# A four-layer graph network on one core: self loops on VectorE, a bank copy ahead of late operands, count maxima and small vector work in other places

## The chip, the core and the metric

The kernel runs on one core of a Trainium2 chip. A core has TensorE (PE, matmuls; PEld are its weight loads), VectorE (DVE), ScalarE (ACT), GpSimd (POOL) and SyncE (SP, which issues DMAs). The metric is the device time of one execution in microseconds (us); lower is better.

## What is computed

`x` has 2048 nodes of 512 features. Four blocks follow one another, each on `relu(layernorm(x))` and added to `x`: an attention block, a block of three GCN layers with self loops and degree scaling, one GCN layer scaled by out degrees, and one layer with edge weights. Cut to what the change touches:

```python
def _gcn_norm(edge_index, n):
    loops = jnp.arange(n)                      # a self loop for each node
    row, col = concat(edge_index[0], loops), concat(edge_index[1], loops)
    deg = segment_sum(ones, col);  dis = rsqrt(deg)
    return row, col, dis[row] * dis[col]
def _gcn_layer(x, row, col, norm, W, b, n):
    h = x @ W
    return segment_sum(h[row] * norm[:, None], col, n) + b
h = relu(_gcn_layer(h, W1, b1));  h = relu(_gcn_layer(h, W2, b2));  h = _gcn_layer(h, W3, b3)
...
h = relu(_layernorm(x));  x = x + relu(segment_sum(norm * (h @ W.T + b)[row], col))
h = relu(_layernorm(x));  x = x + relu(segment_sum((h @ Wx)[col] * edge_weight, row))
```

## The kernel before

Since all edges share one index set, the kernel keeps a dense matrix `count` of how often an edge joins two nodes (16-bit, 128 partitions x 16 tiles x 2048) and turns each segment sum into matmuls with it. After the attention there are five "layers", numbered 0 to 4 in the code: three of the GCN block, the fourth with out degrees, and the one with edge weights.

**Products.** Each layer begins with `products(layer)`: 16 tiles of 128 nodes, each a product with the weights made of 12 matmuls of 128x512 (high and low halves of both operands). For tile t, ACT writes the high half of the input (`split_hi`), DVE the low half (`split_lo`), both into one of two slots of `h_parts`, and PE waits for the low half in `await_parts`, two matmuls before the end of the tile in front of it (in layers 1 and 2). In layer 2 the result is split by ACT and then by DVE (`product_lo`) into `g`. In layers 0 and 1 ACT evicts it to `h_gcn_t` and `operands` makes from it the parts of the half-size products.

**Half-size products.** In layers 0 and 1 the product with `count` is done in two halves h (a pair each) of seven steps of 32 matmuls by a Strassen-like scheme (`paired_sums`). Left operands are `A11`, `A12`, `A22` and the sums `S1` to `S4`, each in two quarters q, each with a high part (`operand_hi`, ACT) and a low part (`operand_lo`, DVE); `combine` (DVE) forms the sums. Right operands are `count` or mixtures of it in `mix` (`mix_two`, `mix_one`, `mix_three`, `mix_four`, DVE). Step 1's banks are copied out by ACT in `keep_first`; step 3 writes into them again and waits for it. `join`, `first_sum`, `second_sum` and `third_sum` (DVE) add banks and multiply by `dis_row`, the in-degree scale of each node. `relu_sums` (ACT) and `largest` (DVE) follow. From the maxima comes a common scale for the next layer: `pair_peak` (DVE) gives a column, `peak_row` (a PE transpose) turns it, `pair_scale` (some 15 tiny DVE instructions) makes powers of two of it, and `peak_all` (a PE matmul) spreads them. The next layer's products have begun by then, and PE meets both in its own queue.

**Sums.** Layers 2 and 3 use plain products with `count` (`sums`), four chunks c of four tiles, each finished by DVE in `finish`.

**Count maxima.** Layer 4 needs the largest entry of `count`, taken tile by tile by `count_peak` on DVE, before `edge_scale` in layer 3's sums.

Every engine runs its own queue in program order and waits on semaphores; all orders are written out by hand. So what stands ahead of an instruction in its queue delays it, whether it needs it or not.

## Time and profile before

| | |
|---|---|
| median of 3 runs | 1406.57 us (1406.09 to 1408.78) |
| the profiled execution's own time | 1407.51 us |
| its span in the trace | 1405.8 us |
| PE busy | 1342.7 us, 96% of the span |
| DVE busy | 952.9 us, 68% |
| ACT busy | 634.5 us, 45% |
| POOL busy | 98.3 us, 7% |

The span runs from the first to the last recorded instruction. The attention ends near 530 us. Layer 0's products run from 532 to 593 us, its half-size products to 698 us; layer 1's to 744 and 847 us; layer 2's products to 901 us and sums to 1022 us; layer 3's products to 1073 us. Matmuls are pipelined and their ends are modelled, so a matmul's printed duration is longer than the distance to the next one.

### The profile page before, as it was taken

To read this page: it belongs to the slowest core of one execution; us is meant where nothing else is said; L and a number is where in the kernel's file an instruction comes from. 1 tells how busy PE (TensorE), PEld (TensorE's weight loads), DVE (VectorE), ACT (ScalarE), POOL (GpSimd) and SP (SyncE) were. 2 spreads that over 40 slices of the span, in tenths; PEclk is the share of its full clock that TensorE was granted. 3 is DMA by queue.
4 is the path that set the end of the run, shared out by engine and by line. 5 is a ranking of instruction groups with operands and counts; after the bars stand their busy time and mean duration, and the time that the engine had idled before them with its cause. 6 is when DMAs were issued, how large, how long until landed. Compare 5 with 4: busy or idle time off the path is not lost.

```text
span 1405.8 us, 26594 instructions
## 1 busy us (share of the span) xinstructions
PE 1342.7 (96%) x11145; PEld 828.3 (59%) x11145; DVE 952.9 (68%) x1374; ACT 634.5 (45%) x1076; POOL 98.3 (7%) x102
## 2 busy tenths in 40 slices
PE   8889999989998998989998998899999999999998
PEld 8779898989996653534443443355444445444443
DVE  8998998999988885678768778833554323532322
ACT  2666566656554456743365434221253224422322
POOL 3120010101002213000000001002100000000000
PEclk9899999999999999999999999999999999999999
DMA  9634334435348721000000012022211222553201
GB/s 338 222 114 148 135 132 137 135 124 175 121 156 285 240 78 47 1 0 30 1 1 1 0 31 83 0 53 83 68 29 39 66 77 71 207 209 105 90 0 60
DMA packets 71333, 136.91 MB, mean 97 GB/s; under 512 B 11908, under 2 KB 24324, under 8 KB 69798
## 3 DMA queue, kind: packets, MB, share of 16 engines
q1 hardware_dynamic: 68542, 123.98, 26.8%
q0 software_dynamic: 1280, 5.77, 1.5%
q10 hardware_dynamic: 1384, 5.38, 1.1%
q8 instruction: 91, 1.49, 0.4%
q14 instruction: 36, 0.29, 0.1%
HBM read 81.79 MB, written 53.32 MB: 96 GB/s over the span
## 4 chain that ended last, share of the span: by engine, by line
PE 73%; DVE 21%; ACT 3%; issue 2%; DMA 1%; POOL 0%; ACTq 0%; DVEq 0%; SPq 0%; POOLq 0%
PE banks L2545 16%; PE banks L2607 11%; PE banks L2485 10%; PE banks L2420 10%; PE banks L1255 6%; PE banks L1659 3%; DVE x_sb L894 3%; PE banks L1192 3%; PE banks L1209 2%; PE banks L1266 2%; PE banks L1166 2%; DVE count_max L3018 2%; DVE x_sb L877 1%; PE banks L2357 1%; PE banks L1629 1%
## 5 line engine op out<-in xcount | busy, mean ns | idle before, releaser
L2420 PE MATMUL banks<-w_parts,h_parts 128*128 128x512 f16 x960 | 221.3, 384 | 15.4 <-DVE h_parts L2695 8.8
L2545 PE MATMUL banks<-g,count 128*128 128x512 f16 x1024 | 227.5, 379 | 0.5 <-DVE tiles L2986 0.5
L2420 PEld LDWEIGHTS banks<-w_parts,h_parts 128*128 128x128 f16 x960 | 91.2, 99 | 134.8 <-DVE h_parts L2695 14.7
L2545 PEld LDWEIGHTS banks<-g,count 128*128 128x128 f16 x1024 | 99.8, 98 | 113.7 <-DVE tiles L2986 1.0
L2607 PE MATMUL banks<-g,part 128*128 128x512 f16 x768 | 165.9, 379 | 0.0
L894 DVE TENSOR_TENSOR x_sb<-eb_parts,x_sb 128x4096 f16<-128x4096 f16 x64 | 145.9, 2279 | 0.0
L1255 PE MATMUL banks<-x_sb 128*128 128x128 f16 x2048 | 126.5, 220 | 12.3 <-DVE x_sb L894 12.2
L1255 PEld LDWEIGHTS banks<-x_sb 128*128 128x128 f16 x2048 | 120.4, 99 | 15.9 <-DVE x_sb L894 14.9
L2607 PEld LDWEIGHTS banks<-g,part 128*128 128x128 f16 x768 | 75.1, 98 | 90.6
L3069 DVE SCALAR_TENSOR_TENSOR part<-count,e_scale,part 128x1024 f16<-128x1024 f32 x29 | 37.2, 1284 | 105.9 <-ACT part L2307 105.9
L2307 ACT ACTIVATE part<-count,e_scale 128x1024 f16<-128x1024 f32 x29 | 33.3, 1149 | 110.9 <-PE banks L2607 110.9
L2697 DVE TENSOR_TENSOR h_parts<-h_gcn_t,h_parts 128x512 f16<-128x512 f32 x48 | 41.1, 862 | 55.4 <-ACT h_parts L2135 55.3
L877 DVE TENSOR_TENSOR x_sb<-iota_src,keys 128x2048 f16<-128x2048 f16 x64 | 77.6, 1213 | 0.0
L2485 PE MATMUL banks<-count,g 128*128 128x512 f16 x256 | 59.6, 392 | 7.7 <-ACT h_gcn_t L2217 7.7
L1266 PE MATMUL banks<-x_sb 128*128 128x64 f16 x1024 | 64.7, 190 | 0.0
L1267 PE MATMUL banks<-x_sb 128*128 128x32 f16 x1024 | 63.8, 177 | 0.0
L2230 ACT ACTIVATE h_gcn_t<-h_gcn_t,b_col,unscale 128x512 f32<-128x512 f32 x32 | 24.7, 807 | 86.4 <-DVE h_gcn_t L2904 44.4
L1266 PEld LDWEIGHTS banks<-x_sb 128*128 128x128 f16 x1024 | 60.4, 96 | 0.5
L1267 PEld LDWEIGHTS banks<-x_sb 128*128 128x128 f16 x1024 | 58.7, 96 | 0.1
L1659 PE MATMUL banks<-wo_sb,att_t 128*128 128x512 f32 x128 | 58.2, 597 | 0.4 <-ACT att_t L1567 0.4
L1006 ACT COPY bias<-banks 128x128 f32<-128x128 f32 x64 | 24.9, 388 | 72.3 <-PE banks L1255 72.2
L2485 PE MATMUL banks<-mix,g 128*128 128x512 f16 x256 | 56.9, 379 | 0.3 <-DVE mix L2809 0.3
(370 smaller groups left out, 2239.6 us busy)
## 6 DMA issues: line engine op xcount, KB each, us to landing
weight_dram<-w_new SPq DMA_DIRECT2D x60, 256.0 KB
count<-weight_dram SPq DMA_DIRECT2D x29, 512.0 KB, 7.0
qk_dram<-stage SPq DMA_DIRECT2D x64, 128.0 KB, 2.4
tiles<-x_dram SPq DMA_DIRECT2D x32, 256.0 KB, 3.5
x_dram<-tiles SPq DMA_DIRECT2D x32, 256.0 KB, 2.8
count<-in_x SPq DMA_DIRECT2D x4, 1024.0 KB, 13.0
h<-in_x SPq DMA_DIRECT2D x16, 256.0 KB, 4.6
h_dram<-h_t SPq DMA_DIRECT2D x8, 512.0 KB, 3.3
```

The costliest lines, as they stand in the source:

```text
L877: dve.tensor_tensor(m.hot_src[:, z].rearrange("p g (c two) -> p g c two", two=2), keep.iota_src[:].rearrange("p (c two) -> p c two", two=2 ...
L894: dve.tensor_tensor(m.hot_eb[:, z].rearrange("p g (t c) -> p g t c", t=NT), values, tiles, ALU.mult).then_inc(s["hots"], 1)
L1192: mm = pe.matmul(out, m.h_slab[slab % 2][:, zh, k, tile * P:(tile + 1) * P], keep.wq[:, zw, k, c * SCOLS:(c + 1) * SCOLS], start=n == 0, s ...
L1255: mm = pe.matmul(m.bias_ps[:, 0:NT * H], m.hot_src[:, z, g], parts[:, part], start=g == part == 0, stop=g == BATCH - 1 and part == 1)
L1266: pe.matmul(m.cw_ps[:, g, 0:2 * CCOLS], m.hot_src[:, z, g], m.hot_cw[:, z, g, 0:2 * CCOLS], start=True, stop=False)
L1267: mm = pe.matmul(m.cw_ps[:, g, CCOLS:2 * CCOLS], m.hot_src[:, z, g], m.hot_cw[:, z, g, 2 * CCOLS:CW], start=False, stop=True)
L1659: mm = pe.matmul(m.wo_ps[:, t % 2], m.att_t[:, k, :], keep.wo[:, k, :], start=k == 0, stop=k == KT - 1)
L2420: mm = pe.matmul(out, m.h_parts[:, slot, zh, k], m.w_parts[:, zw, k], start=n == 0 and layer != 3, stop=n == len(passes) - 1)
L2485: mm = pe.matmul(m.agg_ps[:, bank + d], left, right(i), start=new and i == 0 and z == 0, stop=i == HT - 1 and z == 1, skip_group_check=not ...
L2545: mm = pe.matmul(m.agg_ps[:, b], m.count[:, i, c, block], m.g[:, i, z], start=i == 0 and z == 0, stop=i == NT - 1 and z == 1)
L2607: mm = pe.matmul(m.banks[:, b], m.part[:, n % 3, z, b * P:(b + 1) * P], m.g[:, q, gz], start=q == 0 and (z, gz) == (0, 0), stop=q == NT - ...
L2697: dve.tensor_tensor(out, source, hi, ALU.subtract).then_inc(s["lo"], 1)
```

## The change

The change makes no instruction disappear except POOL's: it moves work between queues and within them.

- The 16 additions of self loops into `count` go from POOL to DVE (`add_loop`), two at each of the first eight tiles of layer 0's products.
- In `keep_first` of the first pair, ACT's copy stands ahead of the high parts of `A22` and `S4` (second quarters), which stood ahead of it.
- `mix_two` of layer 1 goes from tiles 10 and 11 to tiles 3 and 6; in layer 0 from 10 and 11 to 10 and 12. The low part of `A22` goes one tile later.
- `dis_row` is written in node order, so that it is read without a stride.
- In the second pair of layers 0 and 1, the two first input tiles of the next layer are split earlier, on ACT and on DVE; `peak_all` goes from step 4 to step 3.
- In the products of layers 1 and 2, `peak_row` goes from tile 1, matmul 4 to tile 2, matmul 0, and `peak_all` from tile 2, matmul 8 to matmul 11.
- `count_peak`: of 16, 11 stood in layer 2's products and 5 in its sums; now 5, 8, and 3 in layer 3's products.

```diff
-def layers_pool(nc, m, s, attended, ident):
+def layers_pool(nc, m, s, attended):
...
-    for t in LOOP_ORDER:
-        first = 2 * t % GPC
-        diag = m.count[:, t, t // PER].rearrange("p (v g) -> p g v", g=GPC)[:, first:first + 2]
-        pool.tensor_tensor(diag, diag, ident[:].rearrange("p (g v) -> p g v", g=2), ALU.add).then_inc(s["looped"], 1)
...
+    def add_loop(t):
+
+        first = 2 * t % GPC
+        diag = m.count[:, t, t // PER].rearrange("p (v g) -> p g v", g=GPC)[:, first:first + 2]
+        dve.tensor_tensor(diag, diag, keep.ident[:].rearrange("p (g v) -> p g v", g=2), ALU.add).then_inc(s["looped"], 1)
...
+            if layer == 0 and t < HT:
+                for i in (2 * t, 2 * t + 1):
+                    add_loop(LOOP_ORDER[i])
...
-               13: OPERANDS[6:7], 14: OPERANDS[7:8], 15: OPERANDS[8:]}
+               13: OPERANDS[6:7], 14: OPERANDS[7:8], 15: OPERANDS[8:12]}
...
         act.copy(by_graph(nodes(m, h, 0)), bank_pair(m, 2 * h)).then_inc(s["kept"], 1)
+        if h == 0:
+            for name, q in OPERANDS[12:]:
+                operand_hi(layer, name, q)
...
-    return m.dis_row[:, c * COLS:(c + 1) * COLS].rearrange("p (v g) -> p g v", g=GPC).unsqueeze(1).to_broadcast([P, n, GPC, GN])
+    return m.dis_row[:, c * COLS:(c + 1) * COLS].rearrange("p (g v) -> p g v", g=GPC).unsqueeze(1).to_broadcast([P, n, GPC, GN])
...
-            act.wait_ge(s["fin"], done + 1)
-            relu_sums(layer, h, (0, 1))
             if h == 1:
                 split_hi(layer + 1, 0)
                 split_hi(layer + 1, 1)
+            act.wait_ge(s["fin"], done + 1)
+            relu_sums(layer, h, (0, 1))
...
-            if layer in (1, 2) and (t, n) == (1, 4):
+            if layer in (1, 2) and (t, n) == (2, 0):
                 peak_row()
-            if layer in (1, 2) and (t, n) == (2, 8):
+            if layer in (1, 2) and (t, n) == (2, 11):
                 peak_all()
...
-        if (number, i) == ((5, 4) if h == 0 else (4, 4)):
+        if (number, i) == ((5, 4) if h == 0 else (3, 6)):
             peak_all()
...
+        if layer and t in (3, 6):
+            mix_two(layer, 0, t // 6)
...
-            if layer == 2 and 5 <= t < 5 + EARLY_PEAKS:
-                count_peak(t - 5)
+            if layer == 2 and t in (5, 7, 9, 11, 13):
+                count_peak((t - 5) // 2)
+            if layer == 3 and t in (6, 8, 10):
+                count_peak(NT - 3 + (t - 6) // 2)
...
-            for i in ((), (0, 1), (2, 3, 4), ())[c]:
-                count_peak(EARLY_PEAKS + i)
+            for i in ((5, 6), (7, 8, 9), (10, 11, 12), ())[c]:
+                count_peak(i)
```

The first place is DVE's queue at the start of layer 0's products. Before (`h_parts` is the low half of an input tile, `rstd` the variance step of the layer norm):

```order
L1736 TENSOR_SCALAR rstd<-stats_106 128x3
L3071 MEMSET b_ones 33x64
L3073 MEMSET b_ones 1x128 x2
L2697 TENSOR_TENSOR h_parts<-h_gcn_t,h_parts 128x512 x4
L1741 RECIPROCAL rstd<-rstd 128x3
```

and of the change:

```order
L1736 TENSOR_SCALAR rstd<-stats_106 128x3
L3080 MEMSET b_ones 33x64
L3082 MEMSET b_ones 1x128 x2
L2770 TENSOR_TENSOR count<-count,ident 128x2x64 x2
L2696 TENSOR_TENSOR h_parts<-h_gcn_t,h_parts 128x512
L2770 TENSOR_TENSOR count<-count,ident 128x2x64 x2
L2696 TENSOR_TENSOR h_parts<-h_gcn_t,h_parts 128x512
```

Two additions now stand ahead of each of the low halves, from tile 2 on.

The second place is ACT's queue at the end of layer 0's products. The casts (L2174, L2169) are the high parts of operands, `g` that of `A22` and `S_1_0_90` that of `S4`; the copy (L2217, L2213) is `keep_first`. Before:

```order
L2174 CAST S_0_0_88<-h_gcn_t 128x1024
L2174 CAST S_1_0_82<-h_gcn_t 128x1024
L2174 CAST g<-h_gcn_t 128x4x256
L2174 CAST S_1_0_90<-h_gcn_t 128x1024
L2217 COPY h_gcn_t<-banks 128x2x512
L2224 ACTIVATE banks,stats_78<-count 128x1024 x4
```

and of the change:

```order
L2169 CAST S_0_0_88<-h_gcn_t 128x1024
L2169 CAST S_1_0_82<-h_gcn_t 128x1024
L2213 COPY h_gcn_t<-banks 128x2x512
L2169 CAST g<-h_gcn_t 128x4x256
L2169 CAST S_1_0_90<-h_gcn_t 128x1024
L2223 ACTIVATE banks,stats_78<-count 128x1024 x4
```

The copy has moved ahead of the last two casts. The same happens in layer 1.

The third place is DVE's queue in layer 2's products (`g` is `product_lo`, `count_max` is `count_peak`). Before:

```order
L2695 SCALAR_TENSOR_TENSOR h_parts<-h_gcn_t,h_scale,h_parts 128x512
L2765 SCALAR_TENSOR_TENSOR g<-banks,g_scale,g 128x512
L3018 TENSOR_REDUCE count_max<-count 128x1
L2695 SCALAR_TENSOR_TENSOR h_parts<-h_gcn_t,h_scale,h_parts 128x512
L2765 SCALAR_TENSOR_TENSOR g<-banks,g_scale,g 128x512
```

and of the change:

```order
L2694 SCALAR_TENSOR_TENSOR h_parts<-h_gcn_t,h_scale,h_parts 128x512
L2764 SCALAR_TENSOR_TENSOR g<-banks,g_scale,g 128x512
L3027 TENSOR_REDUCE count_max<-count 128x1
L2694 SCALAR_TENSOR_TENSOR h_parts<-h_gcn_t,h_scale,h_parts 128x512
L2764 SCALAR_TENSOR_TENSOR g<-banks,g_scale,g 128x512
L2694 SCALAR_TENSOR_TENSOR h_parts<-h_gcn_t,h_scale,h_parts 128x512
L2764 SCALAR_TENSOR_TENSOR g<-banks,g_scale,g 128x512
L3027 TENSOR_REDUCE count_max<-count 128x1
```

A maximum now follows every second tile, not every tile.

## Rows read from the trace of the kernel before

**Rows 1.** Page, part 1: busy us of each engine (share of the span) and instructions.

```profile
PE 1342.7 (96%) x11145; PEld 828.3 (59%) x11145; DVE 952.9 (68%) x1374; ACT 634.5 (45%) x1076; POOL 98.3 (7%) x102
```

**Rows 2.** PE's waits, whole span: who waits for whom: us, times, longest.

```profile
PE banks L2420 <- DVE h_parts L2695: 8.8, 11, 1.5
...
PE banks L2485 <- DVE mix L2809: 0.3, 2, 0.2
```

**Rows 3.** Timelines, 530 to 549 us, start of layer 0: start, us, instruction [idle before].

```profile
532.77 9.82 POOL L2066 TENSOR_TENSOR count<-count,ident 128x128 f16<-128x128 f16 x16
...
536.46 6.16 DVE L1736 TENSOR_SCALAR rstd<-stats 128x3 f32<-128x3 f32 x1
...
543.13 1.29 DVE L2697 TENSOR_TENSOR h_parts<-h_gcn_t,h_parts 128x512 f16<-128x512 f32 x2
...
543.88 5.12 PE L2420 MATMUL banks<-w_parts,h_parts 128*128 128x512 f16 x12 [5.47 <-DVE h_parts L2697]
```

**Rows 4.** Windows: length; busy of PE, PEld, DVE, ACT, POOL; PE's granted clock, DMA.

```profile
543.88:548.84 4.96, 4.96 (x12) 1.85 (x13) 0.54 (x1) 0.00 (x0) 0.00 (x0) 0.51 0.00 0
762.30:769.21 6.91, 6.91 (x32) 3.14 (x33) 4.62 (x3) 4.44 (x8) 0.00 (x0) 1.00 0.00 0
852.63:857.86 5.23, 5.23 (x18) 1.93 (x16) 4.07 (x15) 0.72 (x1) 4.47 (x4) 0.69 0.93 306
```

**Rows 5.** Timelines of ACT and PE, steps 2 and 3, layers 0 and 1.

```profile
603.12 1.04 ACT L2174 CAST S<-h_gcn_t 128x1024 f16<-128x1024 f32 x1 [0.21 <-DVE h_gcn_t L2778]
...
610.24 1.01 ACT L2217 COPY h_gcn_t<-banks 128x1024 f32<-128x1024 f32 x1
...
611.30 9.86 PE L2485 MATMUL banks<-count,g 128*128 128x512 f16 x32 [3.80 <-ACT h_gcn_t L2217]
...
762.30 7.08 PE L2485 MATMUL banks<-count,g 128*128 128x512 f16 x32 [3.85 <-ACT h_gcn_t L2217]
```

**Rows 6.** Timelines of PE and DVE, first tiles of layer 1.

```profile
698.36 3.83 PE L2420 MATMUL banks<-w_parts,h_parts 128*128 128x512 f16 x17
...
704.03 0.16 DVE L2727 TENSOR_REDUCE peak<-h_max 128x1 f32<-128x5 f32 x1
...
704.24 0.27 PE L2363 MATMUL banks<-ident,peak 128*1 128x128 f32 x1 [2.05 <-DVE peak L2727]
...
706.87 0.75 DVE L2695 SCALAR_TENSOR_TENSOR h_parts<-h_gcn_t,h_scale,h_parts 128x512 f16<-128x512 f32 x1 [0.21 <-ACT h_parts L2133]
```

**Rows 7.** Timelines of PE, ACT and DVE in layer 2's products.

```profile
866.74 2.76 PE L2420 MATMUL banks<-w_parts,h_parts 128*128 128x512 f16 x12 [0.47 <-DVE h_parts L2695]
...
867.45 0.72 ACT L2133 ACTIVATE h_parts<-h_gcn_t,h_scale 128x512 f16<-128x512 f32 x1 [1.94 <-PE banks L2420]
...
869.46 0.74 DVE L2695 SCALAR_TENSOR_TENSOR h_parts<-h_gcn_t,h_scale,h_parts 128x512 f16<-128x512 f32 x1
...
898.36 3.19 PE L2420 MATMUL banks<-w_parts,h_parts 128*128 128x512 f16 x14 [0.75 <-DVE h_parts L2695]
```

**Rows 8.** Timelines of DVE and PE in layer 3's products.

```profile
1042.56 0.75 DVE L2765 SCALAR_TENSOR_TENSOR g<-banks,g_scale,g 128x512 f16<-128x512 f32 x1 [1.11 <-ACT g L2161]
...
1044.26 1.09 DVE L2697 TENSOR_TENSOR h_parts<-h_gcn_t,h_parts 128x512 f16<-128x512 f32 x1 [0.95 <-ACT h_parts L2135]
...
1045.41 0.39 PE L2416 MATMUL banks<-b_parts,b_ones 33*128 33x512 f16 x1 [0.15 <-DVE h_parts L2697]
...
1055.94 0.75 DVE L2765 SCALAR_TENSOR_TENSOR g<-banks,g_scale,g 128x512 f16<-128x512 f32 x1 [1.11 <-ACT g L2161]
...
1058.13 0.39 PE L2416 MATMUL banks<-b_parts,b_ones 33*128 33x512 f16 x1
```

**Rows 9.** DVE's groups by shape, 530 to 910 us: busy us, mean ns.

```profile
L3018 DVE TENSOR_REDUCE count_max<-count 128x1 f32<-128x2048 f16 x11 | 25.0, 2274 | 0.0
...
L2900 DVE TENSOR_TENSOR h_gcn_t<-banks,h_gcn_t 128x1024 f32<-128x1024 f32 x16 | 19.5, 1220 | 6.5 <-PE banks L2485 5.0 <-ACT h_gcn_t L2217 1.5
...
L2904 DVE TENSOR_TENSOR h_gcn_t<-h_gcn_t,dis_row 128x1024 f32<-128x1024 f32 x8 | 16.2, 2021 | 0.3
```

More of the change, by code:

```diff
@@ L1796 @@
 FIN = (0, 10, 20, 20 + NT, 20 + 2 * NT)
-EARLY_PEAKS = 11
 LOOP_ORDER = tuple(range(PER)) + tuple(range(HT, HT + PER)) + tuple(range(PER, HT)) + tuple(range(HT + PER, NT))
@@ L2204, in products @@
                 act.wait_ge(keep.attention_sems["dis_made"], c + 1)
-                act.copy(m.dis_row[:, c * COLS:(c + 1) * COLS], m.agg_ps[:, c]).then_inc(keep.attention_sems["dis_rowed"], 1)
+                act.copy(m.dis_row[:, c * COLS:(c + 1) * COLS].rearrange("p (g v) -> p g v", g=GPC),
+                         m.agg_ps[:, c].rearrange("p (v g) -> p g v", g=GPC)).then_inc(keep.attention_sems["dis_rowed"], 1)
             if layer == 4 and t == 1:
@@ L2790, in mix_two @@
         tiles = slice(PER * part, PER * (part + 1))
+        if layer == 0:
+            dve.wait_ge(s["looped"], HT * (h + 1))
         if h:
@@ L2830, in operands @@
             combine(layer, "S3", 1)
-        if t == 10:
-            if layer == 0:
-                dve.wait_ge(s["looped"], HT)
-            mix_two(layer, 0, 0)
+        if layer == 0 and t in (10, 12):
+            mix_two(layer, 0, t // 12)
         if t == 11:
             operand_lo(layer, "S3", 1)
-            mix_two(layer, 0, 1)
         if t == 12:
@@ L2841, in operands @@
             combine(layer, "S2", 0)
+        if t == 14:
             operand_lo(layer, "A22", 0)
-        if t == 14:
             combine(layer, "S1", 0)
@@ L2948, in paired_sums @@
             mix_three(layer, h, 3)
+            if h == 1:
+                split_lo(layer + 1, 0)
+                split_lo(layer + 1, 1)
             dve.wait_ge(s["joined"], 6 * number + 1)
@@ L2956, in paired_sums @@
                 weight_spread(layer + 1)
-            else:
-                split_lo(layer + 1, 0)
-                split_lo(layer + 1, 1)
             largest(layer, h, "C11")
@@ L2963, in paired_sums @@
             if h == 0:
-                if layer == 0:
-                    dve.wait_ge(s["looped"], NT)
                 mix_two(layer, 1, 0)
@@ L3117, in graph_layers @@
     layers_act(nc, keep, m, s, tools.act)
-    layers_pool(nc, m, s, attended, keep.ident)
+    layers_pool(nc, m, s, attended)
     layers_pe(nc, keep, m, s, tools.pe)
```

## Prediction, made before the change was run

> **What bounds the kernel now.** I read the page first: PE is busy for 96% of the span and no other engine for more than 68% [rows 1]. The change takes no matmul away, so it can only win what PE loses by waiting or by running at the lower clock. The list of PE's waits shows whose these are; the reader should see that DVE's low halves cost 8.8 us in eleven waits, the longest 1.5 us [rows 2]. Then I went through the timelines of the stages that the diff touches, and through windows for the clock. In window 762.30 a step's 32 matmuls start within 6.91 us at full clock [rows 4], 0.216 us each, so a product of 12 takes 2.59 us. Printed idle time begins at a modelled end that lies 0.16 to 0.17 us behind the next possible start, so each wait costs that much more than printed. The waits to look at:
>
> - 5.47 us in layer 0's products [rows 3].
> - 3.80 and 3.85 us for ACT's copy before step 3, layers 0 and 1 [rows 5].
> - 2.05 us for the maximum at the start of layer 1 [rows 6], and its like in layer 2.
> - A wait of 0.75 us before each product of layer 2 [rows 7].
>
> **Self loops.** DVE's variance step, 128x3 numbers, takes 6.16 us and ends at 542.62; POOL's sixteen additions end at 542.59 [rows 3]. DVE was held by POOL, not by its own work, and the low half that PE waits for stands behind it. PE then starts at 543.88 and its 12 matmuls take 4.96 us with a granted clock of 0.51, the lower level of 1.2 GHz [rows 3, 4]: 2.37 us more than 2.59. The place costs 5.64 + 2.37 = 8.0 us. With POOL's additions gone the step is a fraction of a microsecond. Two additions now stand ahead of the low half. No row shows one on DVE. POOL's took 0.61 (9.82/16) [rows 3], the upper bound. By elements alone, at the rate of a multiplication with a strided operand (2.02 us for 1024) [rows 9], it is 0.25, the lower bound, and a fixed part comes on top. I take 0.4, nearer to the vector row, and 0.8 for two. DVE's low half came 0.51 us after the step's end [rows 3]; so it would come at about 536.6 + 0.5 + 0.8 = 537.9 and be done at 538.6, where PE is free at 538.24 (the wait's beginning less the modelled part). **Gain 7.6**, with 7.2 to 7.9 by the bounds. The other fourteen lie in DVE's waits for ACT, in tiles where PE needs 2.59 us and DVE some 2.
>
> A rule bears on the cause. The Trainium skill, "GPSIMD Engine Reference", section 8 (Key points), says that GpSimd shares its SBUF interfaces with VectorE, which clash when VectorE runs in a two-port mode or has two SBUF inputs. The trace agrees as to the first: the held step has one input. By its second half the additions themselves would be safe now that POOL is idle there; the sum is unchanged.
>
> **The copy ahead of late operands.** PE waits for the copy, which ends at 611.25; it stands behind two casts that wait for DVE's sums. The last cast that stays ahead begins at 603.12 and takes 1.04 [rows 5], so the copy can run from 604.2 to 605.2. PE's step 2 ends at 607.34 (611.30 less 3.96), 2 us later: the wait goes whole. What is late next? `A22`'s cast comes after the copy, at 605.2 to 606.2; DVE, busy until then, takes it at 607. The mixture and the join for step 4 follow, needed seven microseconds later. Layer 0: 3.96, and its step 3 takes 9.86 printed where the like one takes 7.08 [rows 5], 2.78 more by the clock. Layer 1: 4.01 and no clock. **Gain 10.7.**
>
> **Mixtures earlier.** The longest wait for a low half, 1.55 us, comes at layer 1's tile behind two mixtures. Two instructions of 1.22 us, moved to tiles with room, leave some 0.2 at each of two places: **gain 1.3**. In layer 0 the move only shifts a wait; nothing.
>
> **Scale chain.** Reading `dis_row` without a stride should bring 2.02 down to the 1.22 of a join of the same shape [rows 9]. Eight such and others shorten DVE's chain at the end of a layer, where DVE is busy throughout. The maximum then comes some 3 us after step 7's end, not at 704.2, which is 5.8 after it (698.36) [rows 6]. PE turns it after 25 matmuls, 5.4 us: no wait. But the chain of tiny instructions keeps its length: from the transpose at 704.24 to the low half of tile 3 at 706.87, which takes 0.75 [rows 6], 3.4 us; 0.4 less without the wait and idle time in it is not sure, so 3.2. PE gets only nine matmuls, 2.0 us, behind the transpose before it needs this low half. A new wait of 1.2 us takes the place of 2.2: **gain 1.0**. In layer 2 the same, and there 16 matmuls of the old row lie in a window at clock 0.69 and take 5.23 [rows 4] where 3.5 is normal: 1.7 more; POOL's bias additions slow DVE there and take some back. **Gain 2.2.** The lower bound is nothing at both, if the new wait grows to the old one. The two small waits for `mix` (0.3 printed) [rows 2], with the modelled part: **0.6**.
>
> **Count maxima.** Ten starts of PE from 866.74 to 898.36 are 3.51 us apart [rows 7], not 2.59: 0.92 lost at each of nine, 0.64 at the first, 8.9. A maximum takes 2.27 [rows 9], about 2.19 start to start. Let PE pass the gate of tile t at 0. ACT starts the next high half at 0.71, DVE could start the low half at 1.46 (0.75 later) and takes 0.74; PE wants it at 2.59. `product_lo` follows at 2.1, a maximum runs from 2.8 to 5.0, so the low half of the tile after next ends at 5.77, wanted at 5.18. A wait of 0.6 then, and the tile without a maximum lets DVE catch up. Five: 3.0. **Gain 5.9.** The eight in the sums lie in waits of 5 us and more.
>
> The three in layer 3 are not free. There `product_lo` starts at 1042.56 and is through at 1043.2; a maximum ends at 1045.4; the low half that began at 1044.26 and took 1.09 ends at 1046.5, and PE, which started at 1045.41, had already waited for it [rows 8]. 1.1 lost, the same at tile 8. At tile 10 the maximum begins at 1056.6 and ends at 1058.8, the low half at 1059.9, against a start at 1058.13 without a wait [rows 8]: 1.8. **Loss 4.0.** Nothing at the one end, 3 x 2.2 = 6.6 at the other.
>
> **Sum.** 7.6 + 10.7 + 1.3 + 1.0 + 2.2 + 0.6 + 5.9 - 4.0 = 25.3. The profiled execution took 1407.51 us (a span of 1405.8 and 1.7 around it), 0.9 above the median of the runs shown. 1407.5 - 25.3 = 1382.2, and on the median's footing 1381.3.
>
> **Rivals.**
>
> *The clock falls elsewhere.* Three of the waits were followed by slow matmuls, 1.7 to 2.8 us each (6.8 in my sum); of the waits of 3.96 and 4.01 us one was and one was not [rows 4, 5]. New waits of 1.2 to 1.8 us stay. If one or two of them meet a fall: 1384 to 1389. Against it: ten waits of 0.75 in a row met none.
>
> The Trainium skill, "TensorE: Matmul & The Clock Gate", Part 1 (What's actually happening), says that the array's default is the throttled state and that work lifts it, judged on a free-running basis. By that rule the same wait may or may not cost, as rows 5 show.
>
> *Maxima hidden.* If DVE has more room than I count, five or all of the waits in layers 2 and 3 are smaller: 3 to 7 us more, 1374 to 1378. For it: the gaps are fractions of a microsecond. Against: each instruction in the count has a row.
>
> *Another wait replaces the copy's.* If the casts now behind the copy hold step 4, 8 of the 10.7 go: 1389 to 1391. Against: 7 us of room.
>
> *No change.* The moves shift waits only. That needs all of the above to fail; 1406.
>
> *Slower.* One mechanism: PE stays at 1.2 GHz behind the short waits left in the products, where ten are (five of 0.6, three in layer 3, two at the scale chain). A product at the lower level costs 2.37 more [rows 3, 4]. It decides from twelve slow products on (25.3 + 2.8 = 28.1): 1409.5 and more. Against it, the trace has eleven waits for low halves [rows 2], and the ten of layer 2 ran at full clock.
>
> **How the numbers follow.** The forecast has 0.60 (1377 to 1386), the clock elsewhere 0.15, maxima hidden 0.13, another wait 0.05, still larger gains 0.02, no change 0.02, slower 0.03. From the forecast's range I reach to most of the clock's cases and to the hidden maxima: 1375 to 1389 holds a little over 8 in 10. A measurement of this kernel can tell about 0.2% (2.8 us) from no change. Faster by more: 0.95; within: 0.02; slower by more: 0.03.
>
> **What would show it.** Right: `rstd`'s step at 0.2 us and no wait of PE behind it; step 3 directly behind step 2 in both layers; multiplications with `dis_row` at 1.22; PE waiting near 1.2 us for tile 3's low half, not for the maximum; five waits of 0.6 in layer 2 and three of 1.1 to 1.8 in layer 3. Wrong: an addition of more than 0.6 us, new windows with a clock under 1.00 behind the new waits, a wait of PE for `joined` before step 4, or layer 3's products no longer than before.

## The result

The changed kernel takes 1385.36 us (median of 4 runs, 1381.71 to 1386.9), the kernel before beside it 1407.67 (4 runs): a ratio of 0.984 (0.981 to 0.986). Run again beside other kernels it took 1384.17 (5 runs), against 1407.65 (9 runs): 0.983 (0.982 to 0.985). The prediction was 1381.3 in a range of 1375 to 1389, with 0.95 on faster by more than 0.2%.

The page's first part of the changed kernel: PE's busy time is 4 us shorter (fewer slow matmuls) and its idle time some 16 us [rows 1].

```profile
PE 1338.9 (97%) x11145; PEld 829.4 (60%) x11145; DVE 944.3 (68%) x1390; ACT 636.0 (46%) x1076; POOL 90.1 (7%) x86
```

PE's waits, whole span of the changed kernel (us, times, longest):

```profile
PE banks L2415 <- DVE h_parts L2696: 4.6, 5, 1.7
PE banks L2419 <- DVE h_parts L2694: 4.4, 7, 1.3
...
PE banks L2419 <- DVE h_parts L2696: 1.3, 2, 0.7
```

The 8.8 us in eleven waits of [rows 2] have become 4.4 in seven, and those for `mix` are gone. The group at L2415, the bias matmul that opens a product of layer 3, has grown to 4.6 us; in the kernel before it was

```profile
PE banks L2416 <- DVE h_parts L2697: 0.6, 4, 0.2
```

The start of layer 0 in the timelines of DVE and PE (start, us, instruction, idle before):

```profile
539.46 0.17 DVE L1736 TENSOR_SCALAR rstd<-stats 128x3 f32<-128x3 f32 x1
540.18 1.30 DVE L2770 TENSOR_TENSOR count<-count,ident 128x128 f16<-128x128 f16 x2
541.10 0.89 DVE L2696 TENSOR_TENSOR h_parts<-h_gcn_t,h_parts 128x512 f16<-128x512 f32 x1
542.05 2.76 PE L2419 MATMUL banks<-w_parts,h_parts 128*128 128x512 f16 x12 [0.56 <-DVE h_parts L2696]
```

`rstd`'s step takes 0.17 us instead of 6.16, PE waits 0.56 instead of 5.47, and its product takes 2.76 instead of 5.12 [rows 3]. Two additions take 0.92 from start to start.

ACT and PE around step 3 of layer 0:

```profile
599.80 1.04 ACT L2169 CAST S<-h_gcn_t 128x1024 f16<-128x1024 f32 x1 [0.22 <-DVE h_gcn_t L2783]
600.76 1.01 ACT L2213 COPY h_gcn_t<-banks 128x1024 f32<-128x1024 f32 x1
601.66 1.05 ACT L2169 CAST g<-h_gcn_t 128x1024 f16<-128x1024 f32 x1
...
603.30 7.07 PE L2484 MATMUL banks<-count,g 128*128 128x512 f16 x32
```

The copy stands behind the cast that was ready, PE's step 3 has no idle time and takes 7.07 where it took 9.86 [rows 5].

The start of layer 1's products, PE and DVE. The maximum is there 3.2 us after step 7's end (687.24), 2.2 before the transpose; the chain of tiny steps then runs to the low half of tile 3, for which PE waits:

```profile
687.24 5.56 PE L2419 MATMUL banks<-w_parts,h_parts 128*128 128x512 f16 x25
690.46 0.16 DVE L2726 TENSOR_REDUCE peak<-h_max 128x1 f32<-128x5 f32 x1
692.63 0.27 PE L2362 MATMUL banks<-ident,peak 128*1 128x128 f32 x1
693.84 0.16 DVE L2638 TENSOR_SCALAR line<-line 1x2 int32<-1x2 int32 x1
694.57 0.22 DVE L2743 TENSOR_SCALAR line<-h_line,line 1x2 f32<-1x2 f32 x1
695.57 0.60 PE L2419 MATMUL banks<-w_parts,h_parts 128*128 128x512 f16 x2 [0.72 <-DVE h_parts L2694]
```

The same place in layer 2, where GpSimd adds biases meanwhile: the second 1x2 step takes 0.65 for 0.22, and PE waits longer.

```profile
833.89 5.58 POOL L2066 TENSOR_TENSOR tiles<-tiles,b_row 128x512 f32<-128x512 f32 x4 [298.01 <-DMA tiles<-x_dram]
834.92 0.26 DVE L2638 TENSOR_SCALAR line<-line 1x2 int32<-1x2 int32 x1
835.75 0.65 DVE L2743 TENSOR_SCALAR line<-h_line,line 1x2 f32<-1x2 f32 x1
837.18 0.60 PE L2419 MATMUL banks<-w_parts,h_parts 128*128 128x512 f16 x2 [1.25 <-DVE h_parts L2694]
```

A maximum in layer 2's products, and the third one in layer 3's, DVE and PE:

```profile
849.43 2.28 DVE L3027 TENSOR_REDUCE count_max<-count 128x1 f32<-128x2048 f16 x1
851.62 0.74 DVE L2694 SCALAR_TENSOR_TENSOR h_parts<-h_gcn_t,h_scale,h_parts 128x512 f16<-128x512 f32 x1
852.42 5.35 PE L2419 MATMUL banks<-w_parts,h_parts 128*128 128x512 f16 x24 [0.43 <-DVE h_parts L2694]
...
1032.86 2.27 DVE L3027 TENSOR_REDUCE count_max<-count 128x1 f32<-128x2048 f16 x1
1035.05 1.06 DVE L2696 TENSOR_TENSOR h_parts<-h_gcn_t,h_parts 128x512 f16<-128x512 f32 x1
1036.17 0.39 PE L2415 MATMUL banks<-b_parts,b_ones 33*128 33x512 f16 x1 [1.72 <-DVE h_parts L2696]
1036.49 4.45 PE L2419 MATMUL banks<-w_parts,h_parts 128*128 128x512 f16 x12
```

In each the low half stands directly behind the maximum and PE behind it. Behind the 1.72 us the twelve matmuls start over 4.38 us instead of 2.7; the window of them, in which the third number from the end is PE's granted clock, 0.62:

```profile
1036.49:1040.94 4.45, 4.45 (x14) 1.58 (x13) 1.27 (x2) 0.00 (x0) 0.00 (x0) 0.62 0.00 0
```

The two groups by shape on DVE that the prediction priced (530 to 890 us; busy us, mean ns):

```profile
L2770 DVE TENSOR_TENSOR count<-count,ident 128x128 f16<-128x128 f16 x16 | 10.4, 844 | 0.0
...
L2915 DVE TENSOR_TENSOR h_gcn_t<-h_gcn_t,dis_row 128x1024 f32<-128x1024 f32 x8 | 9.8, 1225 | 0.3
```

(Instructions without a wait between them overlap as printed, so 844 is not the distance between two additions.) The multiplication takes 1.225 us instead of 2.021 [rows 9].

Where the time went, by stages. Each length is the distance from PE's first matmul of the stage to that of the next one, in the timeline of one profiled execution (the bias matmul of 0.32 us that opens layer 3's products counts to the sums ahead of it); "again" is the changed kernel's second profile.

| stage | before | after | again | gain | predicted |
|---|---|---|---|---|---|
| layer 0, products | 61.33 | 54.21 | 54.21 | 7.1 | 7.6 |
| layer 0, steps | 104.84 | 97.76 | 97.75 | 7.1 | 6.7 + 0.3 |
| layer 1, products | 46.11 | 43.32 | 43.32 | 2.8 | 1.3 + 1.0 |
| layer 1, steps | 102.10 | 97.75 | 97.75 | 4.35 | 4.0 + 0.3 |
| layer 2, products | 54.82 | 47.07 | 48.84 | 7.75; 5.98 | 2.2 + 5.9 |
| layer 2, sums | 121.25 | 121.24 | 121.24 | 0.0 | 0 |
| layer 3, products | 50.47 | 56.21 | 54.52 | -5.74; -4.05 | -4.0 |
| all of these | 540.92 | 517.56 | 517.63 | 23.4; 23.3 | 25.3 |

What lies ahead is untouched and varies: the first product started at 532.19 before, 535.27 after and 530.87 again, and between 530.2 and 533.1 in the profiles of the experiments. What lies behind layer 3's products took 332.7, 332.8 and 332.7 us. So a single execution's time can stand some 3 us off for reasons outside the change, and in what follows the verdicts rest on stages where less than that is asked.

### The profile page after: what moved, and what is told of

The parts are those of the page before. It is cut to its first block, busy times and chain, and to the rows that moved or that the text cites. A ratio compares the mean times of both kernels' runs of the same rounds, so it can differ in the third digit from the quotient of the medians.

```text
span 1385.6 us, 26596 instructions
## 1 busy us (share of the span) xinstructions
PE 1338.9 (97%) x11145; PEld 829.4 (60%) x11145; DVE 944.3 (68%) x1390; ACT 636.0 (46%) x1076; POOL 90.1 (7%) x86
## 4 chain that ended last, share of the span: by engine, by line
PE 81%; DVE 13%; ACT 3%; issue 2%; DMA 1%; POOL 0%; ACTq 0%; DVEq 0%; SPq 0%; POOLq 0%
PE banks L2544 16%; PE banks L2484 14%; PE banks L2606 12%; PE banks L2419 11%; PE banks L1255 6%; PE banks L1659 4%; DVE x_sb L894 3%; PE banks L1192 3%; PE banks L1209 2%; PE banks L1266 2%; PE banks L1166 2%; DVE count_max L3027 1%; PE banks L2356 1%; DVE x_sb L877 1%; PE banks L1629 1%
## 5 line engine op out<-in xcount | busy, mean ns | idle before, releaser
L2484 PE MATMUL banks<-mix,S 128*128 128x512 f16 x256 | 56.8, 379 | 0.0
```

Of the source, the lines that this page charges most:

```text
L2484: mm = pe.matmul(m.agg_ps[:, bank + d], left, right(i), start=new and i == 0 and z == 0, stop=i == HT - 1 and z == 1, skip_group_check=not ...
```

## Experiments

"Before +" and "after +" say which of the two kernels was edited. Stage lengths are measured as above.

**The copy alone (before +).**

```diff
-               13: OPERANDS[6:7], 14: OPERANDS[7:8], 15: OPERANDS[8:]}
+               13: OPERANDS[6:7], 14: OPERANDS[7:8], 15: OPERANDS[8:12]}
...
         act.copy(by_graph(nodes(m, h, 0)), bank_pair(m, 2 * h)).then_inc(s["kept"], 1)
+        if h == 0:
+            for name, q in OPERANDS[12:]:
+                operand_hi(layer, name, q)
```

> The kernel before with one edit: ACT's copy of step 1's banks ahead of the high parts of A22 and S4 (second quarters), in layers 0 and 1. My theory: the two waits of PE for the copy (3.96 and 4.01 us with the modelled part) go whole and the slow matmuls behind the first of them too, so layer 0 from step 1 to step 4 takes 20.7 us instead of 27.48 and layer 1 20.7 instead of 24.74; 10.8 us in all, 0.992 of the time before. Rival one: the casts now behind the copy hold step 4 or later, so that less than 3 us is left and the difference shows as a new wait in steps 4 to 7 (77.36 us before in each layer). Rival two: the clock falls at the same place without the wait, layer 0 then takes 23.5 us.

Measured: 1396.81 us (4 runs) against 1408.2 (7 runs), ratio 0.991 (0.988 to 0.994). The steps of layer 0 went from 104.84 to 98.08, those of layer 1 from 102.10 to 98.08; every other stage is within 0.25 of before. The waits for the copy are gone and none takes their place: 10.8 us by the two stages. The medians differ by 11.4, and the ratio's interval is 8.6 to 16.8 us. It is the largest part of the change, in four lines.

**Self loops back on GpSimd (after +).**

```diff
+    for t in LOOP_ORDER:
+        ...
+        pool.tensor_tensor(diag, diag, ident[:].rearrange("p (g v) -> p g v", g=2), ALU.add).then_inc(s["looped"], 1)
...
-            if layer == 0 and t < HT:
-                for i in (2 * t, 2 * t + 1):
-                    add_loop(LOOP_ORDER[i])
```

> The changed kernel with the sixteen self loops back on POOL at their old place. My theory: DVE's variance step (128x3) is held until POOL's last addition ends, about 6 us instead of 0.17, PE's wait in front of its third product grows from 0.56 to about 5.5 us and slow matmuls follow; from the first product of layer 0 to the start of the fourth 17.5 us instead of 10.26, everything else as in the changed kernel, so about 7.3 us more. Rival: the step was long because of what stood around it on DVE and ACT, not because of POOL; then the step stays at 0.2 us and the stage at 10 to 11 us.

Measured: 1388.07 us in one run; layer 0's products 60.52 instead of 54.21, 6.3 more (about 7.3 expected). Timelines of GpSimd, DVE and PE:

```profile
531.92 9.79 POOL L2065 TENSOR_TENSOR count<-count,ident 128x128 f16<-128x128 f16 x16
...
535.58 6.15 DVE L1736 TENSOR_SCALAR rstd<-stats 128x3 f32<-128x3 f32 x1
...
543.00 4.19 PE L2423 MATMUL banks<-w_parts,h_parts 128*128 128x512 f16 x12 [5.45 <-DVE h_parts L2700]
```

The hold is back, to the end of GpSimd's run of additions, as in [rows 3]; only the slow matmuls behind it cost 1.4 us this time where they had cost 2.4. Layer 3's products took 54.53 here: the three waits and no slow product.

**Self loops on GpSimd, but after the second product (after +).** As before, with one more line ahead of the loop.

```diff
+    pool.wait_ge(s["prod"], 2)
     for t in LOOP_ORDER:
```

> The changed kernel with the self loops on POOL, but started only when two products of layer 0 are done, so that they lie behind DVE's variance step. My theory: what counts is the overlap with a DVE step that has one input in SBUF, not the engine that adds. The variance step takes 0.2 us, PE's wait of 0.56 goes to near zero, DVE's low halves are slower while POOL works (about 1.0 us instead of 0.69), and the reciprocal of 128x3 behind them is held until POOL's end. First product to fourth 9.5 to 10.5 us, the whole within 1 us of the changed kernel. Rival: sixteen additions on POOL cost PE some 7 us wherever they stand while layer 0's products run; 1.5% of nothing saved, 7 us more than the changed kernel.

Measured: 1384.08 us in one run; layer 0's products 53.47, 0.7 less than the changed kernel's 54.21. GpSimd and DVE:

```profile
539.32 10.04 POOL L2066 TENSOR_TENSOR count<-count,ident 128x128 f16<-128x128 f16 x16 [5.70 <-PE banks L2424]
...
546.02 0.96 DVE L2701 TENSOR_TENSOR h_parts<-h_gcn_t,h_parts 128x512 f16<-128x512 f32 x1 [2.66 <-ACT h_parts L2135]
546.91 0.16 DVE L1741 RECIPROCAL rstd<-rstd 128x3 f32<-128x3 f32 x1
```

What was to be avoided was the meeting of `rstd`'s TENSOR_SCALAR with the additions, not GpSimd as such: with the run elsewhere PE doesn't wait for its third product at all, since no additions stand ahead of the low half. I had expected the RECIPROCAL on the same 128x3 numbers to be held in its turn. It wasn't: 0.16 us in the middle of the run. The low halves, with two inputs, took up to 0.96 instead of 0.69 beside it.

**Node order alone (before +).**

```diff
-    return m.dis_row[:, c * COLS:(c + 1) * COLS].rearrange("p (v g) -> p g v", g=GPC).unsqueeze(1)...
+    return m.dis_row[:, c * COLS:(c + 1) * COLS].rearrange("p (g v) -> p g v", g=GPC).unsqueeze(1)...
...
-                act.copy(m.dis_row[:, c * COLS:(c + 1) * COLS], m.agg_ps[:, c])...
+                act.copy(m.dis_row[:, c * COLS:(c + 1) * COLS].rearrange("p (g v) -> p g v", g=GPC),
+                         m.agg_ps[:, c].rearrange("p (v g) -> p g v", g=GPC))...
```

> The kernel before with one edit: dis_row in node order. My theory: its multiplications take 1.22 us instead of 2.02 and 0.69 instead of 1.09, DVE's chain at the end of layers 0 and 1 gets 2.4 us shorter, and PE's wait of 2.05 us (2.2 with the modelled part) for the maximum goes in both; with the transpose at its old place the low half of tile 3 comes in time as well, so layer 1's first three products end 8.4 us after step 7, not 10.5, and layer 2's 8.4 to 9, not 12.2. 4.4 to 6 us in all. That would be as much as the changed kernel gets there (1.7 and 2.9) although it moved the transpose as well. Rival: the chain is bound by ACT's relus and PE's steps; then the multiplications are shorter but the maximum comes less than 1 us earlier and PE's wait stays over 1 us.

Measured: 1404.03 us in one run; layer 1's products 44.08 (46.11 before), layer 2's 52.27 (54.82). DVE and PE, start of layer 1 (step 7 ended at 698.10):

```profile
701.73 0.16 DVE L2728 TENSOR_REDUCE peak<-h_max 128x1 f32<-128x5 f32 x1
...
701.95 0.27 PE L2364 MATMUL banks<-ident,peak 128*1 128x128 f32 x1
```

The maximum comes at 3.6 us instead of 5.7 [rows 6], and PE doesn't wait for it even with the transpose at its old place. So the order of nodes alone brings 2.0 and 2.55 us, which is more than the whole chain brought in layer 1 in the change (below).

One stage got longer without an edit in it: layer 1's steps took 103.46 us (102.10 before). PE's wait for the copy is that of before, but this time its step 3 was slow:

```profile
760.00 8.77 PE L2486 MATMUL banks<-count,g 128*128 128x512 f16 x32 [3.85 <-ACT h_gcn_t L2218]
```

It took 7.08 behind the same wait in [rows 5], so the wait that the prediction priced without slow matmuls can have them too.

**Strided order again (after +).** The reverse edit.

> The changed kernel with the in-degree scale written and read in the old, strided order again; nothing else is changed. My theory (with the transpose later, the maximum has slack): the multiplications take 2.02 us again instead of 1.22, the maximum of layer 1 comes about 1.5 us later (4.7 instead of 3.2 us after step 7's end), still ahead of the transpose at 5.4, and the products of layers 1 and 2 stay at 43.3 and 47.1 us, the steps at 97.8: no change of more than 0.3. Rival: the order is what brought the gain at the end of the layers: the transpose waits again, and each of the two stages is 1 to 3 us longer.

Measured: 1381.12 us in one run; layer 1's products 43.82 (43.32), layer 2's 47.52 (47.07; 48.84 again), the steps 97.75. The multiplications took 2.02 us as expected, but there is a new wait. DVE and PE:

```profile
686.52 0.16 DVE L2725 TENSOR_REDUCE peak<-h_max 128x1 f32<-128x5 f32 x1
686.59 0.74 DVE L2693 SCALAR_TENSOR_TENSOR h_parts<-h_gcn_t,h_scale,h_parts 128x512 f16<-128x512 f32 x1
...
687.39 0.82 PE L2418 MATMUL banks<-w_parts,h_parts 128*128 128x512 f16 x3 [0.30 <-DVE h_parts L2693]
```

The transpose doesn't wait, as I had said, but tile 2's low half stands behind the maximum in DVE's queue and is now late: 0.5 us in layer 1. My expectation of no change over 0.3 missed that by 0.2, the rival's 1 to 3 us by more. With the later transpose the order of nodes is worth 0.5 us in layer 1; with the old one 2.0. Layer 2 has the new wait too (0.32), but its stage differs by more than that among kernels that do the same there (47.07 to 48.91), so its length settles nothing. The two edits cover the same wait, and where both are made the later transpose only makes the chain end later.

**The transpose six matmuls earlier, the spreading four (after +).**

```diff
-            if layer in (1, 2) and (t, n) == (2, 0):
+            if layer in (1, 2) and (t, n) == (1, 6):
                 peak_row()
-            if layer in (1, 2) and (t, n) == (2, 11):
+            if layer in (1, 2) and (t, n) == (2, 7):
                 peak_all()
```

> The changed kernel with the transpose of the maximum six matmuls earlier (tile 1, matmul 6; it was tile 2, matmul 0) and the spreading four earlier (tile 2, matmul 7). Theory (the chain's length from the transpose is fixed, so PE's wait for tile 3's low half shrinks by what the transpose is earlier, 1.3 us, as long as the maximum is there): layer 1's products 43.3 to 42.4, the wait of 0.72 gone; layer 2's 47.1 to 45.8, the wait of 1.25 at 0.2 or less. Rival (the maximum is not there yet): a wait of PE for the maximum comes in its place and the stages stay at 43.3 and 47.1.

Measured: 1379.86 us in one run. Layer 1's products 42.43, no wait left; layer 2's 46.34, with two waits, 0.56 for the chain and 0.20 for the low half, in place of the 1.25 or 2.1. As the theory has it in layer 1 (42.4), 0.5 short of it in layer 2 (45.8). The transpose at tile 2, matmul 0 was later than the maximum needs.

**Three maxima out of layer 3's products (after +).**

```diff
-            if layer == 3 and t in (6, 8, 10):
-                count_peak(NT - 3 + (t - 6) // 2)
...
+            if layer == 2 and c and b == 1:
+                count_peak(12 + c)
```

> The changed kernel with the three count maxima of layer 3's products moved into layer 2's sums, one in each of the last three chunks; those of layer 2's products stay. Theory: the three maxima are the whole loss of layer 3's products: they take 50.5 us (before: 50.5), instead of 56.2, and layer 2's sums stay at 121.2. Rival (the loss has another part, such as split work moved there, or the maxima cost as much in the sums): layer 3's products stay over 51.5, or the sums grow by over 1 us.

Measured: 1378.72 us in one run; layer 3's products 50.47, layer 2's sums 121.24. Four starts of PE at L2415 still show 0.15 to 0.16 of idle time, as in [rows 8], and none more. The loss in layer 3 was the three maxima and what followed them, nothing else.

**All sixteen in layer 2's sums (after +).** The five of layer 2's products go too: three behind each of the first three chunks, seven inside the last three.

> The changed kernel with all 16 count maxima in layer 2's sums, none in the products. Theory: layer 2's products go from 47.1 to about 43.9 (five waits of 0.42 to 0.75 printed go, each with 0.16 of the modelled end), layer 3's from 56.2 or 54.5 to 50.5, sums stay 121.2. Rival (a maximum in the sums delays finish): sums over 122 and layer 3's first products later.

Measured: 1377.33 us in one run. Layer 3's products 50.47 and sums 121.25 as expected. Layer 2's products 45.97, not 43.9: the wait for tile 3's low half was 2.18 in this execution and the matmuls behind it were slow (the first 34 took 8.77 us at a granted clock of 0.81, where they take 7.51 at 1.00). The comparison of the two kernels with the earlier transpose, with and without the five maxima (46.34 here above, 43.10 below), is free of that: 3.24 us for the five.

**Both together (after +).** All sixteen in the sums, transpose and spreading earlier.

> The changed kernel with all 16 count maxima in layer 2's sums and none in the products of layers 2 and 3, and with the transpose of the maximum at tile 1, matmul 6 and the spreading at tile 2, matmul 7. My theory (what is left of the loss is DVE's maxima ahead of low halves, and the scale chain counted from the transpose): layer 3's products 50.5 us instead of 56.2 (three waits and one slow product gone), layer 2's products about 3.0 to 3.3 shorter by the maxima and 1 to 1.4 by the chain (43 us), layer 1's products 0.9 shorter (42.4), layer 2's sums unchanged at 121.2; together 9 to 11 us below the changed kernel where its clock fell, 8 to 9 where it did not: a median near 1376, ratio to before 0.977. Rival: the maxima are not free in the sums either (16 x 2.2 us on DVE, with finish behind them), so the sums grow by 2 us or more and the total stays above 1380.

**The changed kernel again, in the same group of runs.**

> The changed kernel itself, unchanged, beside the others on the same chip. Theory: 1382 to 1386, ratio 0.982 to 0.985; layer 3's products are 54.5 us (three waits alone) or 56.2 (with one slow product): by the theory that the clock's fall comes and goes from execution to execution, either may stand here. Rival: the fall belongs to this kernel and stands there each time (56.2).

Measured: both together 1373.83 us (5 runs), ratio to before 0.976 (0.975 to 0.978); the changed kernel 1384.17, ratio 0.983. Layer 1's products 42.43, layer 2's 43.10, sums 121.24, layer 3's products 50.48. A median of 1376 was expected: 2 us better than that.

In the changed kernel's second profile layer 3's products took 54.52, so the slow product of the first belongs to an execution, not to the kernel. Layer 2's products took 48.84, 1.8 more than in the first. DVE and PE there:

```profile
830.51 1.08 DVE L2638 TENSOR_SCALAR line<-line 1x2 int32<-1x2 int32 x1
...
833.60 0.60 PE L2419 MATMUL banks<-w_parts,h_parts 128*128 128x512 f16 x2 [2.08 <-DVE h_parts L2694]
...
834.65 8.92 PE L2419 MATMUL banks<-w_parts,h_parts 128*128 128x512 f16 x34
```

The 1x2 step took 1.08 us, not 0.26, the wait grew by as much, and the 34 matmuls behind it took 8.92 against 7.86. What decides it is how far GpSimd's additions have come when the step is due. GpSimd at that moment:

```profile
830.31 1.26 POOL L2066 TENSOR_TENSOR tiles<-tiles,b_row 128x512 f32<-128x512 f32 x1
```

This addition ends at 831.57, the step, which began at 830.51, at 831.59. In the first profile an addition ran from 833.89 to 835.16 and the step from 834.92 to 835.18: it came up near the addition's end. In each of the twelve profiles that have the additions beside this step, it ends within 0.03 us of the end of an addition, after 0.26 to 1.19 us. The second 1x2 step ends with the next addition and takes 0.65 each time. The first profile's 0.26 was the exception among the changed kernel and those edits of it that leave the transpose in place: the wait of PE was 1.25 us there, 1.82 in one and 2.08 to 2.18 in five others. This led to the last two kernels.

**GpSimd's first four bias additions after layer 2's products (after +).**

```diff
+    pool.wait_ge(s["prod"], 3 * NT)
     for t in range(NT):
         b = t % PER
         pool.wait_ge(s[f"in_x{b}"], 16 * (t // PER + 1))
         pool.tensor_tensor(m.tiles[:, b], m.tiles[:, b], m.b3_row[:], ALU.add).then_inc(s["plus"], 1)
```

> The changed kernel, but GpSimd's first four bias additions (5.6 us, which begin 5.2 to 5.6 us after layer 2's products) wait until those products are done; they are needed some 20 us after that. Theory (these additions hold DVE's tiny one-input steps on 1x2 numbers, 0.65 for 0.22 and up to 1.2 for 0.16 us, and so make PE's wait at tile 3 of layer 2 1.25 to 2.1 us instead of layer 1's 0.72): the two steps take 0.16 and 0.22 us, the wait is 0.72, and layer 2's products take 46.3 to 46.6 us (47.1 to 48.8 with the additions there); the sums stay at 121.2. Rival (what stretches the chain in layer 2 is something else, such as its own instructions or a DMA): the steps stay long and the wait over 1.2.

Measured: 1382.78 us in one run. Layer 2's products 45.94 (47.07 and 48.84). DVE, PE and GpSimd:

```profile
832.02 0.16 DVE L2639 TENSOR_SCALAR line<-line 1x2 int32<-1x2 int32 x1
...
832.74 0.22 DVE L2744 TENSOR_SCALAR line<-h_line,line 1x2 f32<-1x2 f32 x1
...
833.74 0.61 PE L2420 MATMUL banks<-w_parts,h_parts 128*128 128x512 f16 x2 [0.72 <-DVE h_parts L2695]
...
871.66 4.95 POOL L2067 TENSOR_TENSOR tiles<-tiles,b_row 128x512 f32<-128x512 f32 x4 [338.69 <-PE banks L2420]
```

Both steps as short as in layer 1, and the wait to the hundredth that of layer 1. The stage is 0.4 us below the 46.3 to 46.6 expected: the `g_scale` step (128x16 numbers, right behind the chain) took 0.17 us as in layer 1, where the changed kernel's took 1.18, and the 34 matmuls behind the wait took 7.51 instead of 7.86. The sums stayed at 121.25. Layer 3's products took 56.11, with a slow product behind the 1.72 again.

**The same with both improvements.**

> The version with all maxima in the sums and the earlier transpose, and GpSimd's first four bias additions after layer 2's products. Theory: layer 2's products take 42.2 to 42.5 us like layer 1's 42.43 (43.10 with the additions there), all else the same: a median of 1373 to 1374 us, which 3 rounds can't tell from 1373.83; the stage can. Rival: the additions run into the sums' first finish instead and layer 2's sums grow past 121.5.

Measured: 1371.06 us (4 runs, 1370.29 to 1371.77) against 1407.9 (7 runs), ratio 0.974 (0.972 to 0.976). Layer 2's products 41.96, the shortest of all and 0.2 under what was expected; sums 121.25, layer 3's products 50.51. The median is 2 us under the 1373 to 1374 expected. After the chain PE shows no idle time:

```profile
830.15 0.38 PE L2370 MATMUL banks<-line,ones 1*128 1x8 f32 x2
830.47 34.71 PE L2420 MATMUL banks<-w_parts,h_parts 128*128 128x512 f16 x160
```

The profiled executions of the two versions took 1373.25 and 1370.85 us. Of these 2.4 us, 1.1 are in this stage and 1.3 ahead of the first product (530.89 against 532.23), where nothing was changed; so 1.1 is what the edit is shown to bring. It is the fastest version found: 13 us below the changed kernel, by nothing but places in queues.

## Why the prediction was right, point by point

The forecast was 1381.3 and the medians 1385.4 and 1384.2. 1.1 us of the difference is its footing (1406.57 of three runs; nine gave 1407.65), 2.0 are terms: 1407.65 - 23.3 = 1384.4. The first median lies 1.0 above that, in a group whose four runs differ by 5.2.

The two profiles miss the 25.3 by the same 2.0, but not by the same term. In the first it is nearly all the slow product behind a maximum in layer 3 (1.7), in the second the scale chain in layer 2 (2.1). That they agree is luck.

- **Self loops**, 7.6 predicted. The first three products take 10.26 us instead of 17.52: 7.26. The wait left is 0.56 printed; an addition costs 0.46 and not 0.4, and the low half behind two of them took 0.89 instead of 0.69. 0.14 went at a later tile. That GpSimd's additions held DVE's step is shown by putting them back and by putting them elsewhere.
- **The copy**, 10.7 predicted, 10.8 alone. Slow matmuls were put at 2.8 behind the wait in layer 0 and at nothing in layer 1; the node-order kernel had 2.9 and 1.7. What I said would be late next, `A22`'s cast and the mixture for step 4, was not.
- **Mixtures and chain in layer 1**, 1.3 + 1.0 predicted, 2.8 measured. No wait is left at the mixtures' new tiles. The node-order kernel, which has the wait behind the mixtures and no other, takes 44.08, the one without any wait 42.43: 1.65. The chain's part is then 1.15. Both parts are differences between kernels; the mixtures were not moved alone, nor were the two earlier splits and the earlier `peak_all` of the half-size products, so their shares stay open. The new wait, 0.72 printed and 0.89 with the modelled part, is worth what the earlier transpose gained, 0.89. Its size was put at 1.2: the chain from the transpose to the end of the low half was put at 3.2 us and took 2.9 (692.63 to 695.51).
- **The chain in layer 2**, 2.2 predicted with nothing as the lower bound. From the shortest length of this stage, 41.96, before lost 12.86, of which 8.9 to the maxima; the changed kernel lost 5.11, of which 3.26 to its five waits (2.46 printed and five times 0.16). Chain and slow matmuls went from 4.0 to 1.85: a gain of 2.1. In the second profile the same subtraction (6.88, less 2.93) leaves 3.95 and no gain at all. Over the seven profiles with GpSimd's additions and the transpose in place, it leaves a gain of 2.1 once, 1.4 to 1.6 twice and none four times. So the 2.2 fits the first profile by luck, and the lower bound, nothing, is the commoner case. I wrote that the bias additions "take some back" without pricing how long one of them holds a 1x2 step.
- **Small mix waits**, 0.6 predicted, 0.65 (97.76 against the copy alone's 98.08, twice). They are gone with the order of nodes alone, and stay gone with the old order in the changed kernel, so more than one of the edits removes them.
- **Maxima in layer 2**, 5.9 predicted. 8.9 before; 3.24 after, by the pair of kernels with and without them: 5.7. Five waits of 0.6, as written (0.43 printed, 0.59 with the modelled part); in the first profile one of them was 0.75 printed, where `g_scale` was held.
- **Maxima in layer 3**, -4.0 predicted (1.1, 1.1, 1.8). The waits are 1.29, 1.29 and 1.72 printed, where 0.15 stood at the first two before; the stage lost 4.05, and 1.7 more where one product was slow. The kernel without them shows all of it.

Of the rivals, *the clock falls elsewhere* came true at one place in the first profile (1.7 us behind the 1.72 us wait) and at another in the second (behind the 2.08). *Maxima hidden* is refuted by the two kernels with maxima moved, *another wait* by the copy alone, *no change* and *slower* by the result.

The rule of the Trainium skill that the prediction weighed, on GpSimd's shared interfaces, agrees with the runs that moved GpSimd's additions. More closely fits the Trainium skill's "SBUF — State Buffer", "Who interferes with whom": a DVE instruction in a two-port mode and a GpSimd instruction lock one another out for a whole instruction, `tensor_scalar` has such a mode, and a reduction never contends. Here every held step was a TENSOR_SCALAR (6.15 us on 128x3, up to 1.19 on 1x2) or had two inputs (`g_scale`, 1.18 us at 838.33 in the changed kernel, 0.17 in layer 1), and the one-element steps, the RECIPROCAL and the reductions kept their time. The 1x2 steps ended with GpSimd's instruction, as the Trainium skill has it. The 128x3 step did not: it lost not one addition but the ten that were still to come of the run. Where they differ the measurement decides; no run here tells why.

## What stays open

Which wait is followed by slow matmuls. The same wait of 1.72 us in layer 3 stands in seven executions (the changed kernel twice and five of the experiments); two of them had a slow product behind it (56.21 and 56.11 us), the others 54.52 to 54.53. Of nine waits of 2.05 to 2.18 us for the maximum or the scale chain, six had slow matmuls behind them, all six in layer 2. Of four waits of 3.80 to 3.85 us for the copy, three had (2.8, 2.9 and 1.7 us). Behind the wait of 5.45 to 5.49 us in layer 0 all four executions that have it had one (before, the copy alone, node order alone, loops back on GpSimd), at 1.4 to 2.5 us. No run here tells what decides it. Nor was the share of the untouched attention in the spread of the times looked into.

## What to carry to other kernels

Work that is off the critical path is free only where the queue that it joins has room: the same maximum cost 0 in the sums, 0.65 between products of layer 2 and 1.1 to 1.8 in layer 3, and of two edits of one chain in layer 1 the order of nodes gave 2.0 us alone, and the whole chain 1.15 with the later transpose. Look at what another engine runs while a chain of tiny instructions is due, since one meeting costs more than the chain's own step. And price a wait with what may follow it: 1.4 to 2.9 us of slow matmuls, in some executions.

## What the hardware showed that I had not expected

- A TENSOR_SCALAR on two numbers took 0.16 us alone and, beside GpSimd's additions of 128x512, 0.26, 0.32, 0.83 or 1.08 to 1.19, always up to the end of an addition; on one number it took 0.13 to 0.14 throughout. The additions suffered too: four of them took 5.58 us there and 4.95 in the sums.
- A RECIPROCAL on 128x3 took 0.16 us in the middle of a run of GpSimd additions that had held a TENSOR_SCALAR of that shape for 6.15 us.
- ACT reads PSUM with a stride as fast as without one when it writes `dis_row` (0.56 to 0.61 us in both orders), while DVE's multiplication with the strided SBUF operand took 2.02 us against 1.22.
